# Two expert stages: routed batches go through the router in two pairs, and the order of the 42 units and of their helper steps changes

## What is computed

```python
x = x + _L0_attn_a_ref(_layernorm(x), ...)
x = x + _L0_ffn_ref(_layernorm(x), router_w, w1, w2)
x = x + _L0_attn_b_ref(_layernorm(x), ...)
x = x + _L0_ffn_ref(_layernorm(x), router_w, w1, w2)

def _L0_ffn_ref(x, router_w, w1, w2):          # E = 8 experts, K = 2 of them for each token
    logits = tokens @ router_w.T
    topv, topi = jax.lax.top_k(logits, K)
    w = jax.nn.softmax(topv, axis=-1)
    gate = jnp.zeros((T, n_experts)).at[jnp.arange(T)[:, None], topi].add(w)
    for e in range(n_experts):
        h = jax.nn.gelu(tokens @ w1[e].T, approximate=False)   # 128 -> 256
        out = out + gate[:, e:e + 1] * (h @ w2[e].T)           # 256 -> 128
```

## Time and profile before

| | us |
|---|---|
| median of 3 runs | 1209.43 |
| lowest, highest | 1206.67, 1224.84 |
| the profiled execution, its own time | 1211.13 |
| span of that profile | 1209.3 |
| TensorE busy in the span | 996.0 (82%) |
| mean granted TensorE clock | 0.909 of full speed |

### The profile page before, as it was taken

One profiled execution on the slowest core, in us unless ns is written; L12 is line 12 of the kernel. 1 busy time (PEld: TensorE's weight loads), 2 busy tenths in 40 slices (PEclk: granted clock), 3 DMA queues, 4 the chain that ended last, 5 costly groups with the idle time before them and its releaser, 6 DMA issues. The chain is left out here.

```text
span 1209.3 us, 18136 instructions
## 1 busy us (share of the span) xinstructions
PE 996.0 (82%) x5906; PEld 657.1 (54%) x5906; DVE 750.6 (62%) x1863; ACT 567.7 (47%) x1029; POOL 449.1 (37%) x606
## 2 busy tenths in 40 slices
PE   4888888977788699277789989998998977887992
PEld 1223323324677599234456655655665646776991
DVE  3778998994455222368787887887775734551222
ACT  1234444433533133177666676776665644332330
POOL 1445555651255166313112231222221222551662
PEclk9789998998889899688798999999999999788996
DMA  9940000000000343248887878787678100003443
GB/s 350 288 139 1 0 0 0 1 1 1 9 28 29 94 139 104 79 126 280 221 239 206 212 200 200 202 200 207 143 198 184 41 1 10 28 28 95 143 127 118
DMA packets 70920, 141.25 MB, mean 117 GB/s; under 512 B 12010, under 2 KB 38385, under 8 KB 69040
## 3 DMA queue, kind: packets, MB, share of 16 engines
q1 hardware_dynamic: 64176, 131.14, 39.3%
q0 software_dynamic: 4608, 8.47, 2.2%
q10 hardware_dynamic: 2048, 0.53, 0.2%
HBM read 82.09 MB, written 63.11 MB: 120 GB/s over the span
## 5 line engine op out<-in xcount | busy, mean ns | idle before, releaser
L1532 POOL TENSOR_SCALAR_AFFINE_SELECT attn_probs<-attn_probs 128x512 f32<-128x512 f32 x128 | 87.7, 720 | 286.6 <-ACT attn_probs L1350 286.6
L1614 DVE TENSOR_REDUCE attn_maxima<-attn_ps_p 128x1 f32<-128x512 f32 (+3 forms) x235 | 145.9, 637 | 55.6 <-PE attn_ps_p L1097 49.3
L2321 DVE SCALAR_TENSOR_TENSOR x_rows<-moe_ps_y,moe_gates,x_rows 128x128 f32<-128x128 f32 x256 | 72.1, 344 | 148.2 <-PE moe_ps_y L2015 148.0
L2092 ACT ACTIVATE moe_hidden<-moe_ps_h 128x512 f32<-128x512 f32 x168 | 91.3, 596 | 76.9 <-PE moe_ps_y L2015 74.5
L1092 PE MATMUL attn_ps_p<-attn_stack 96*128 96x384 f32 (+3 forms) x341 | 116.1, 382 | 8.7 <-DVE attn_maxima L1614 8.7
L674 POOL TENSOR_TENSOR rwkv_rs<-rwkv_recept,rwkv_state 128x512 f32<-128x512 f32 x64 | 76.0, 1187 | 104.8 <-DVE rwkv_state L756 102.2
L1140 PE MATMUL attn_ps_q<-attn_stack 128*128 128x128 f32 (+3 forms) x343 | 105.4, 371 | 6.3 <-DMA attn_stack<-attn_neg_max 4.8
L2148 POOL DMA_INDIRECT expert_results<-moe_weighed,moe_blocked x80 | 78.6, 983 | 74.1 <-DVE moe_weighed L2311 64.0
L756 DVE TENSOR_TENSOR_SCAN rwkv_state<-rwkv_decay,rwkv_kv 128x512 f32<-128x512 f32 x64 | 91.5, 1430 | 3.2
L1614 DVE TENSOR_REDUCE attn_maxima<-attn_ps_t 128x1 f32<-128x384 f32 (+3 forms) x117 | 74.5, 636 | 30.1 <-PE attn_ps_t L1097 28.3
L2015 PEld LDWEIGHTS moe_ps_y<-value,moe_hidden 128*128 128x128 f32 x672 | 86.2, 203 | 3.1
(11 more groups left out here) (297 smaller groups left out, 2195.2 us busy)
## 6 DMA issues: line engine op xcount, KB each, us to landing
attn_kept<-parts SPq DMA_DIRECT2D x32, 768.0 KB, 4.7
attn_stack<-attn_kept SPq DMA_DIRECT2D x128, 192.0 KB
moe_buffer<-in_pad SPq DMA_DIRECT2D x2, 8320.0 KB, 49.5
attn_stack<-attn_kept SPq DMA_DIRECT2D x128, 96.0 KB
value<-attn_values SPq DMA_DIRECT2D x35, 256.0 KB, 4.9
moe_blocked<-moe_buffer SPq DMA_DIRECT2D x80, 65.0 KB, 1.9
moe_w_of<-experts_in_w SPq DMA_DIRECT2D x40, 128.0 KB, 2.1
moe_w_of<-value SPq DMA_DIRECT2D x40, 128.0 KB, 2.1
```

The source lines that it names most:

```text
L1532: nc.gpsimd.affine_select(out=tile, in_=tile, compare_op=ALU.is_ge, fill=0.0, base=0, pattern=[[0, 4], [1, P]], channel_multiplier=-1).the ...
L1614: nc.vector.tensor_reduce(maxima[:, u % 2, h:h + heads, t], tiles, AX_X, ALU.max).then_inc(g_free, 1)
L2092: fn(hidden[:, u % 2, k * T:(k + 1) * T], ps_h[u % 2][k][:], ACT.Gelu).then_inc(gelu_done, 1)
L2321: last = stt(x[:, at:at + P], ps_y[u % 2][:, t * C:(t + 1) * C], gates[:, j, t, e:e + 1], x[:, at:at + P], ALU.mult, ALU.add)
```

## The change

Line numbers of the changed kernel differ from those of the kernel before, since the router and the block table have moved into classes of their own (`Router`, `BlockTable`) with tiles of their own.

1. Order of units: 24 dense units, then five times two sparse and one dense, then three dense. Before: 21 dense, then ten times one sparse and one dense, then one dense. The sparse units stand in slots 24, 25, 27, 28, 30, 31, 33, 34, 36, 37 instead of 21, 23, ..., 39.
2. The four routed batches are handled as two pairs of eight 128-row tiles. The norm, finding, choosing, ranking and placing are one call for a pair, with wider instructions; scaling, transposing and routing stay one call for each half pair. The pairs have their own tiles, so they and the dense batches no longer wait for each other's.
3. Lags. A dense batch begun at slot `DENSE_AT[c]`: scale in lag 2, `turn` in lag 3, `route` in lag 4, `choose` in lag 5. Pairs: `turn` in slots 1, 2, 7, 8, `route` one later, `find` in 3 and 9, `choose` in 4 and 10, `rank` and `place` in 5 and 11, the table in 12 (before: the table in slot 11).
4. The statistics of the first pair stand at the head of DVE's stage, ahead of `low_x(0)`; the second pair's in slot 3. In moe0 two of the four pieces of the rounding of the first weights move into slots 0 and 1.
5. `w1_of` and `weighed` get 16 slots like `blocked`; `HELD` is gone. The only wait of a load for a free slot is now that of 16 blocks back.
6. The four fetches of `combined` get a semaphore each, and no longer wait for each other.
7. `FOLLOWING_AT` goes from 20 to 26; `scale_of` of the dense batches 2 and 3 stand behind sends 8 and 24.

```diff
-ROUTED = (0, 3, 4, 1, 5, 6, 2, 7)
-BEGIN = (0, 0, 1, 4, 5, 6, 9, 12)
-LAST_SPARSE = 5
-SCALED_BEHIND = {4: 1, 5: 3, 6: 9, 7: 15}
-FOLLOWING_AT = 20
-SEQUENCE = "D" * 21 + "SD" * 10 + "D"
+PAIR = 2 * TC
+DENSE_AT = {1: 2, 2: 9, 3: 17}
+PAIR_TURN = (1, 2, 7, 8)
+PAIR_STATISTICS = 3
+PAIR_SCALE = (6, 7)
+COUNT_AT = 12
+SCALED_BEHIND = {2: 8, 3: 24}
+FOLLOWING_AT = 26
+SEQUENCE = "D" * 24 + "SSD" * 5 + "DDD"
...
-SLOTS, HELD = 16, 8
-BATCH_SENT = 2 * TC * 16
+SLOTS = 16
...
                 if n % AT_ONCE == 0:
-                    rows_at = read_table(nc.sync, row_i, n, NE * REGION)
-                    columns_at = read_table(nc.sync, column_i, n, (NE - 1) * HC * P)
-                if n >= HELD and n % GROUP == 0:
-                    sp.wait_ge(up_done, HC * (AT[n // GROUP - 2] + 1))
+                    rows_at = read_table(nc.sync, table.row_i, n, NE * REGION)
+                    columns_at = read_table(nc.sync, table.column_i, n, (NE - 1) * HC * P)
                 if n >= SLOTS:
+                    if n % GROUP == 0:
+                        sp.wait_ge(up_done, HC * (AT[(n - SLOTS) // GROUP] + 1))
                     sp.wait_ge(*returned_by(n - SLOTS))
...
-                sp.dma_start(combined[:, i], source).then_inc(fetched, 16)
-                if i + 1 < NS:
-                    sp.wait_ge(fetched, 16 * (i + 1))
+                sp.dma_start(combined[:, i], source).then_inc(fetched[i], 16)
...
             for u in range(NU):
-                for c in due(1, u):
-                    turn(c)
-                for c in due(4, u):
-                    if is_sparse[c]:
-                        rank(c)
-                for c in due(2, u):
-                    route(c)
-                if u == COUNT_AT:
-                    count_rows()
+                for r in pair_due(3, u):
+                    rank_pair(u, r)
+                if u == COUNT_AT:
+                    count_rows(u)
+                for n in half_due(1, u):
+                    route_pair(u, n)
+                for c in due(4, u):
+                    route(c)
+                for n in half_due(0, u):
+                    turn_pair(n)
+                for c in due(3, u):
+                    turn(c)
...
-            for c in range(1, NC_):
-                if c not in SCALED_BEHIND:
-                    scale_of(c)
...
+            pairs.scale_on_pool(pool, 0)
+            pairs.prepare_on_pool()
+            table.prepare_on_pool()
+            scale_of(1)
+            pairs.scale_on_pool(pool, 1)
+            for n in range(4 * PAIR):
+                send(n)
+                for c in SCALED_BEHIND:
+                    if SCALED_BEHIND[c] == n:
+                        scale_of(c)
...
+                if u == PAIR_STATISTICS:
+                    pairs.statistics(v, 1)
```

More of the change, by code:

```diff
@@ L1792, in returned_by @@
     def returned_by(n):
-        return returned[n % HELD], round_before * BLOCKS // HELD * 16 + 16 * (n // HELD + 1)
+        earlier = round_before * len(range(n % SLOTS, BLOCKS, SLOTS))
+        return returned[n % SLOTS], 16 * (earlier + n // SLOTS + 1)
     with ExitStack() as ctx:
@@ L1889, in _ @@
                     store(DENSE[j])
[L1890 removed]
+            for n in range(BLOCKS - SLOTS, BLOCKS):
                 sp.wait_ge(*returned_by(n))
@@ L2101, in _ @@
                 loads.wait(act)
-                for n in range(PIECES):
-                    round_w1(n)
+                round_w1(0)
+            pairs.scale(act, 0)
+            if ready is None:
+                round_w1(1)
             for u in range(NU):
@@ L2332, in add @@
                 tt(rows_of, rows_of, one, ALU.add).then_inc(added, 1)
+            pairs.statistics(v, 0)
             low_x(0)
```

560 lines of the change are left out of this document (340 added, 220 removed).

## The result

| | before | after |
|---|---|---|
| median, us | 1208.05 (4 runs, 1204.1 to 1224.84) | 1168.49 (4 runs, 1166.43 to 1178.72) |
| ratio | | 0.969, 95% interval 0.962 to 0.976 |
| the profiled execution: its time, span | 1211.13, 1209.3 | 1178.72, 1177.0 |
| up to A's start | 290.6 | 295.2 |
| A, to the attention's first transposes | 220.9 | 202.3 |

A forecast was written before the change was run, and what follows sets the result against it. PE's own work bounded the middle, POOL's last send the head's end. A's -16.3 and B's -22.1 us gave -38.4; with 2 held back, 1211.1 became 1174.7, and 1.7 above the median meant 1173 us, range 1155 to 1197.

The forecast's parts named there:

- A: The first expert stage, starting at 290.6 us before the change; predicted to change by -16.3 us.
- Head: Stage part up to the first group of blocks; last send hangs on slot 17, starting at 83.0 and 82.0 us.
- B: The second expert stage, starting at 986.5 us before the change; predicted to change by -22.1 us.
- G: PE's transpose of the first group's last blocks, ending the head; predicted 21.7 us earlier in A, 21.0 in B.
- Middle: Stage part from G on, to the first fetch; predicted loss of 12.4 us in A and 5.9 in B.
- The loop: Return and load reusing 16 block slots, 12.2 us against 7.6 hidden; PE waits 4.6 us in slots 27, 30, 33.
- First return to first new load 4.25 us: Step between a group's first return and the first load reusing its slot; 4.25 of the loop's 12.2 us.
- Each wait is followed by a slow slot that costs 1.3 us: Behind PE's six new waits in the middle, up products at half speed cost 1.3 us more each.
- The first return of A: In A, POOL's first return waits for the attention's norm step, coming at 25.1 instead of 18.9 us after G.
- Fetches: At each stage's end, four result fetches issued at once take 9 us, 7 us less per stage.
- Sum: Over both stages: -16.3 us in A and -22.1 in B, together -38.4.
- the reserve of 2: 2 us held back from the sum for small waits in the heads that had not been found.

The follow-up runs named there:

- 24 slots: The changed kernel with 24 instead of 16 slots for blocks, their first weights and their weighed results; 1138.07 us.
- the two profiles: The changed kernel without any edit, profiled in two separate sets of runs; medians 1168.49 us and, the second time, 1166.15 us.

## Why the prediction was right, and where it was not

**Head: right.** Slot 17 starts 70.7 us into A and 70.0 into B (70.6 and 69.6 predicted), the last send starts at 83.6 and 82.9 (83.0 and 82.0), G is at 93.9 and 93.1 (94.1 in A; 21.0 earlier in B, measured 21.8). One reading under the forecast for B was wrong: the 1089.53 of the earlier trace rows is the last send but one. POOL's timeline of the kernel before has one more:

```profile
1090.88 0.96 POOL L2138 DMA_INDIRECT moe_buffer<-moe_sent,moe_index  x1 [0.17 <-issue]
```

From the last send to G it was therefore 10.5 us in B before, not 11.9. With the right row the same sum gives G 22.4 us earlier in B instead of 21.0; the 21.8 measured lies between the two. POOL's wait for the first dense statistics between sends was 6.6 us, more than the "little" of the prediction, and for the second 2.6. I had foreseen that the last send hangs on the second, and moving it alone moved the last send by all of its 4 us. PE's wait for the first group was 7.5 us instead of 9.

**Middle: the mechanism right, its size too large.** The loop was named as the cause, and 24 slots remove it. PE's waits in slots 27, 30 and 33 of B were 3.7, 2.6 and 2.2 us instead of 4.6 each, the first one of A 8.2 instead of about 11. B lost 2.9 us instead of 5.9 (4.0 if the first profile is averaged with the second), A 9.8 to 11.3 instead of 12.4. Two terms were off:

- *First return to first new load 4.25 us*. It is 2.4 for group 6 (1109.52 to 1111.89). The rows did not measure this step. In the kernel before, the first load of group 4 also waits (by `HELD`) until the up product of the unit two groups back is done, and that ended last, at 427.84, 0.4 us ahead of the load at 428.25. A row of PE's timeline in A before, and one of SP's waits behind G:

```profile
425.89 1.95 PE L1989 MATMUL moe_ps_h<-moe_blockT,moe_w_of 128*128 128x128 f32 x16
```

```profile
SPq L1884 <- PE moe_ps_h L1989: 8.7, 5, 2.7
```

  Point 5 of the change takes this wait away, so the prediction charged the changed kernel for a wait that it no longer has. Group 4 came at G + 29.1 all the same (29.4 predicted), since its four loads took 6.5 us from the first issue to the last instead of 4.2: the fourth was issued 3.0 us behind the third instead of 1.3. Groups 6 and 8 came at G + 46.0 and 61.7 instead of 46.5 and 63.6.
- *Each wait is followed by a slow slot that costs 1.3 us.* Behind the first group and group 4 it cost 1.4 to 2.8 in the two profiles (slots of 4.7 to 6.1 us against 3.3). Behind groups 6 and 8 of B it came in one profile and not in the other, each time for only one of the two groups; in A it came behind group 6 both times and behind group 8 never. That the sum of the middle came out only a few us too large is thus partly luck.

The smaller waits for the second group of a pair (0.7 us in slot 25, 1.2 in slot 31) were in the sum only for groups 1 and 9.

The rule of the Trainium skill that I cited ("TensorE: Matmul & The Clock Gate", the part on thin M) says that a loop which waits for a DMA in each round lets the clock fall in each round. The traces agree behind the first group and group 4, where PE waited 3.7 to 8.2 us in all, and not behind every later wait. The run that keeps PE busy up to the last block shows that the slow slot comes from PE's wait.

**The first return of A: right.** The norm step stood at G + 23.5, the first return at G + 24.7 (25.1 predicted); with the statistics in slot 21 it is 18.4 (18.9).

**Fetches: right.** 9.1 us, as the sum had it. The formula of the Trainium skill ("DMA: Bandwidth & Descriptors", Anatomy of one DMA) gave an estimate of 6.8. The page fits it to single DMAs that GpSimd issues, and these four come from SP's queue, so it was carried over to a case that it does not cover. Here the third of the four was only added at 7.7 us behind the first issue, so the estimate is too low.

**Sum.** -18.6 for A and -25.8 for B against -16.3 and -22.1: the stages are 6.0 us better than the sum, 8.0 with the reserve of 2. In the profiled execution that was outweighed by 12.1 us in code that did not change, so it took 1178.7 where the sum gives 1174.7. The median lies 4.5 us below the forecast.

**What the prediction did not see.** It booked the new order as a loss behind G (5.9 us in B, 12.4 in A, the saved 9.5 us of three dense slots already counted), and the runs agree that the order gives nothing with 16 slots. It did not go on to say that the order is then not worth having without more buffer slots, and that one group more of them turns it into a gain.

## What to carry over

When the order of work is changed so that consumers come in pairs, count the slots between the release of a buffer and its next use before and after: buffers that were enough for the old order can take the whole gain away, and the trace before shows it only as a distance, not as a wait. A latency read between two rows can hold a wait for something else, here one that the change itself removes: look up what released the second row before you use it as a price. And where several chains meet (a dense batch's statistics between the sends of the routed ones), move the step of the less urgent chain behind the urgent one's last instruction: it gave 4 us in each stage here and cost nothing.

## What the runs showed of the hardware

- Short waits can bring the clock down too: with PE busy until 4.6 us before the last block, four waits of 0.7 to 1.0 us for single blocks were followed by up products 0.43 us apart at a granted clock of 0.54 (nearly all of it the lower level, 1.2 GHz). With one wait of 0.8 us they stood 0.23 us apart at 1.00 (2.4 GHz). In the first case the clock still read 1.00 through the waits and fell when PE was at work again.
- Equal waits, unequal outcome: two waits of 1.35 and 1.12 us, one behind the other, were followed by a slot of 3.3 us at 1.00 in one execution of the changed kernel and by one of 6.0 us that began at 0.50 in another.
- POOL's pow over 128x8 took 1.63 us, over 128x4 1.04: twice the width cost 57% more time.
- Of four fetches of 512 KB issued within 2.0 us the last was added 9.1 us behind the first issue. One alone took 3.84, and four one behind the other 15.8.
